# SiLU written into its PSUM bank, and GpSimd making the rests of divided down products, in a cross-attention and mixture-of-experts kernel

## The reference

```python
# x (8, 256, 128), ctx (8, 256, 96), float32; D = 128, 8 experts + 1 shared, top 2
x = x + xattn(layernorm(x), ctx)         # sim = q k^T, normalised over the whole (q, k) plane of a batch,
                                         # softmax over k, times value, times Wo^T
h = layernorm(x)
probs = softmax(h @ gate_w + gate_b); topk_probs, topk_idx = top_k(probs, 2)
cw = sum(one_hot(topk_idx, 8) * topk_probs[..., None], axis=2)
def swiglu(v): a, b = split(v, 2); return silu(a) * b
shared = swiglu(h @ sw1 + sb1) @ sw2 + sb2
routed = sum_e cw[..., e] * (swiglu(h @ rw1[e] + rb1[e]) @ rw2[e] + rb2[e])
x = x + shared + routed
```

## Time and profile before

| | |
|---|---|
| median of 3 runs | 134.9 us (134.72 to 135.77) |
| the profiled execution | 135.15 us, its span 133.4 us |
| TensorE, VectorE, ScalarE, GpSimd busy | 96%, 81%, 64%, 18% of the span |
| granted TensorE clock | full in every slice (2.4 GHz) |

### The profile page before, as it was taken

The page is one execution under the profiler, slowest core; times in us unless marked ns, Lnnn a source line. Parts: engine busy times, 40 slices in busy tenths (PEclk is TensorE's granted clock), DMA queues, the critical chain, the costliest instruction groups (busy, mean ns, idle before and its releaser), DMA issues.

```text
span 133.4 us, 2135 instructions
## 1 busy us (share of the span) xinstructions
PE 127.5 (96%) x632; PEld 96.7 (72%) x632; DVE 107.6 (81%) x313; ACT 84.8 (64%) x165; POOL 23.9 (18%) x41
## 2 busy tenths in 40 slices
PE   7899999889999999999999999999999999999992
PEld 7677796858577776686788676598677667788871
DVE  1497788696997989999759997699697879989872
ACT  1557978996265389947653299956633987647250
POOL 7184154057700020602100020001200000000000
PEclk9999999999999999999999999999999999999999
DMA  3999400002910000098000002087000207910022
GB/s 107 304 331 269 149 7 0 0 2 86 337 59 0 0 0 2 10 296 328 0 5 0 0 0 79 18 292 332 2 0 0 79 5 182 403 44 5 0 79 79
DMA packets 8828, 12.97 MB, mean 97 GB/s; under 512 B 1321, under 2 KB 6994, under 8 KB 8306
## 3 DMA queue, kind: packets, MB, share of 16 engines
q1 hardware_dynamic: 8242, 12.62, 28.1%
q10 hardware_dynamic: 576, 0.23, 0.6%
HBM read 11.73 MB, written 1.11 MB: 96 GB/s over the span
## 4 chain that ended last, share of the span: by engine, by line
PE 61%; issue 15%; DVE 9%; ACT 7%; POOL 6%; DVEq 0%; POOLq 0%; ACTq 0%
PE bank L998 55%; ACT prob L508 3%; POOL w_rest L434 3%; POOL ln_rstd L419 2%; PE bank L1062 1%; PE bank L1014 1%; ACT L553 1%; PE bank L1113 1%; PE bank L1090 1%; DVE x L902 1%; ACT act_head L580 1%; PE bank L1181 1%; DVE g_beats L824 1%; DVE g_rank L827 1%; ACT silu L588 1%
## 5 line engine op out<-in xcount | busy, mean ns | idle before, releaser
L588 ACT ACTIVATE silu<-bank,b_cols 128x512 f32<-128x512 f32 (+1 forms) x37 | 24.8, 676 | 23.7 <-PE bank L998 23.2
L998 PE MATMUL bank<-x_head,w_head 128*128 128x512 f32 x72 | 33.7, 468 | 0.3 <-issue 0.3
L998 PE MATMUL bank<-x_head,w_rest 128*128 128x512 f32 x72 | 28.5, 395 | 0.0
L998 PE MATMUL bank<-x_rest,w_head 128*128 128x512 f32 x72 | 28.5, 395 | 0.0
L881 DVE SCALAR_TENSOR_TENSOR act<-bank,b_cols,silu 128x512 f32<-128x512 f32 (+1 forms) x34 | 24.9, 734 | 1.3 <-DVE silu L873 0.3
L873 DVE TENSOR_TENSOR silu<-silu,cw_all 128x512 f32<-128x512 f32 (+1 forms) x28 | 18.6, 668 | 3.3 <-ACT silu L588 2.6
L998 PE MATMUL bank<-act,w_sb 128*128 128x512 f32 x38 | 19.4, 592 | 0.0
L998 PEld LDWEIGHTS bank<-x_head,w_head 128*128 128x128 f32 x72 | 13.6, 189 | 5.3 <-issue 2.7
L998 PEld LDWEIGHTS bank<-x_rest,w_head 128*128 128x128 f32 x72 | 13.6, 189 | 3.9 <-issue 1.9
L998 PEld LDWEIGHTS bank<-x_head,w_rest 128*128 128x128 f32 x72 | 13.5, 188 | 3.3
L890 DVE TENSOR_TENSOR act_rest<-act,act_head 128x512 fp32r<-128x512 f32 x15 | 10.0, 685 | 4.1 <-ACT silu L588 2.0
(11 more groups left out here) (130 smaller groups left out, 219.4 us busy)
## 6 DMA issues: line engine op xcount, KB each, us to landing
cw_all<-cw_dram SPq DMA_DIRECT2D x4, 1024.0 KB, 7.0
cw_all<-cw_dram SPq DMA_DIRECT2D x4, 512.0 KB, 5.0
cw_all<-cw_dram SPq DMA_DIRECT2D x6, 256.0 KB, 3.7
x_sb<-in_x_dram SPq DMA_DIRECT2D x4, 256.0 KB, 4.2
w_sb<-in_L_ffn_rw_dram SPq DMA_DIRECT2D x1, 1024.0 KB, 7.4
ctx_sb<-in_ctx_dram SPq DMA_DIRECT2D x4, 192.0 KB, 4.2
out_dram<-x SPq DMA_DIRECT2D x3, 256.0 KB, 2.1
w_sb<-in_L_ffn_rw_dram SPq DMA_DIRECT2D x1, 512.0 KB, 7.1
```

The costliest lines, as they stand in the source:

```text
L588: scalar.activation(silu[:, k, cols], hid(n, 0)[:, cols], ACT.Silu, bias=b1_cols[:, 0, e:e + 1]).then_inc(silu_sb, 1)
L998: return pe.matmul(dst, lhs, rhs, start=start, stop=stop, skip_group_check=True)
```

## The change

- SiLU of stages 4 to 8, and of stages with e >= 2 in the later chunks but the last stage, is written back into the PSUM bank that it was read from (in_bank); the weighting reads it there and writes the SBUF tile. TensorE's a half of stage n then waits for the weighting of stage n - 2, and no longer for its SiLU only. In the first routed expert of chunks 1 to 3, the b half times SiLU is written into its own bank, and the weighting reads that.
- The divided stages become 25: 4, 6, 7, 8; 9 to 13, 15, 16, 17; 18, 20, 21, 22, 24, 25, 26; 27 to 32 as before. Ten are new: 4, 6, 7, 12, 13, 15, 20, 21, 22, 24.
- For the 19 of them below 27, GpSimd makes the rest, in two instructions of 256 columns each. Before some of them it waits for a piece of VectorE's work (clear_of_vector). The six others stay on VectorE.
- Their heads are made in stage m + 2 ahead of that stage's SiLU; those of stages 7, 16 and 25 inside cw_copy, between cw_rows and cw_t.
- w2's heads are made in stage 2, w2's rests on GpSimd in stage 3. The first variance's power moves two slots later, the scores' power one slot and place.

```diff
-        POOL_AT = {'first_rstd': [-9, 1], 'scores_rstd': [-2, 0], 'second_rstd': [4, 0]}
+        POOL_AT = {'first_rstd': [-7, 1], 'scores_rstd': [-1, 1], 'second_rstd': [4, 0]}
...
+        DIVIDED_OF = [(4, 6, 7, 8), (0, 1, 2, 3, 4, 6, 7, 8), (0, 2, 3, 4, 6, 7, 8), range(NX - STRAIGHT - 1)]
+        DIVIDED = [n for n in range(NX * C) if n % NX in DIVIDED_OF[n // NX]]
+        BY_POOL = [n for n in DIVIDED if n < NX * (C - 1)]
+        BY_DVE = [n for n in DIVIDED if n not in BY_POOL]
+        WITH_WEIGHTS = [m for m in DIVIDED if m < NX * (C - 1) and m % NX == E - 1]
...
+            return m + 2 if m < NX * (C - 1) else m + 1
...
+        def in_bank(n):
+            return FOUR_BANKS_FROM <= n < LAST and n % NX >= (1 if n < NX else 2)
...
+            def clear_of_vector(m):
+                c, e = m // NX, m % NX
+                if e in (1, 2):
+                    pool.wait_ge(shift_sb, c + 2)
+                elif e == 4 and c + 2 < C:
+                    pool.wait_ge(simstat_sb, c + 3)
+                elif e == 4:
+                    pool.wait_ge(gz_sb, C)
+                elif e == 6:
+                    pool.wait_ge(cw_sb, c + 2)
+
+            def act_rests(m):
+                pool.wait_ge(act_head_sb, divided(m))
+                for cols in (slice(0, N // 2), slice(N // 2, N)):
+                    pool.tensor_tensor(act_rest[:, m % 3, cols], act[:, m % 4, cols], act_head[:, m % 3, cols].bitcast(F32), ALU.subtract).then_inc(pool_rest_sb, 1)
...
+                if n == 3:
+                    pool.wait_ge(shift_sb, 2)
+                    pool.wait_ge(scaled_sb, weighted(n))
+                    w2_rests()
+                if n - 1 in BY_POOL:
+                    clear_of_vector(n - 1)
+                    act_rests(n - 1)
...
+                    if NX * c - 2 in WITH_WEIGHTS:
+                        act_heads(NX * c - 2)
...
-                    scalar.activation(silu[:, k, cols], hid(n, 0)[:, cols], ACT.Silu, bias=b1_cols[:, 0, e:e + 1]).then_inc(silu_sb, 1)
+                    silu_out = hid(n, 0)[:, cols] if in_bank(n) else silu[:, k, cols]
+                    scalar.activation(silu_out, hid(n, 0)[:, cols], ACT.Silu, bias=b1_cols[:, 0, e:e + 1]).then_inc(silu_sb, 1)
...
-                for m in divided_in(n, ("first",)):
+                for m in heads_in(n, True):
                     act_heads(m)
                 if n >= 2:
                     expert_silu(c, e)
...
-                if n in (5, 6):
-                    w2_heads(n - 5)
+                if n == 2:
+                    w2_heads(0)
+                    w2_heads(1)
...
-                        dve.tensor_tensor(silu[:, k, cols], silu[:, k, cols], cw_all[:, e - 1, cols], ALU.mult).then_inc(scaled_sb, 1)
+                        dve.tensor_tensor(silu[:, k, cols], hid(n, 0)[:, cols] if in_bank(n) else silu[:, k, cols], cw_all[:, e - 1, cols], ALU.mult).then_inc(scaled_sb, 1)
...
-                    for m in divided_in(n, ("first", "between")):
+                    for m in dve_rests_in(n):
                         act_rests(m)
...
-                    pe.wait_ge(silu_sb, n - 1)
+                    if in_bank(n - 2):
+                        pe.wait_ge(scaled_sb, weighted(n - 2))
+                    else:
+                        pe.wait_ge(silu_sb, n - 1)
...
-                    pe.wait_ge(w2_rest_sb, 1)
-                    pe.wait_ge(act_rest_sb, divided(n))
+                    pe.wait_ge(w2_rest_sb, len(W2_GROUPS))
+                    if n in BY_POOL:
+                        pe.wait_ge(pool_rest_sb, 2 * (BY_POOL.index(n) + 1))
+                    else:
+                        pe.wait_ge(act_rest_sb, BY_DVE.index(n) + 1)
```

More of the change, by code:

```diff
@@ L307, in xattn_moe_kernel, with heads_in, dve_rests_in, weighted @@
         DOWN_BEHIND, CLOSE_FROM = 3, NX * (C - 1) + 1
-        DIVIDED = [n for n in range(NX - 1, LAST - STRAIGHT)
-                   if n >= NX * (C - 1) or n % NX in ((0, 1, 2, 7, 8) if n < NX * 2 else (0, 7, 8))]
-        def parts_slot(m):
[L313 to L323, removed]
+        DIVIDED_OF = [(4, 6, 7, 8), (0, 1, 2, 3, 4, 6, 7, 8), (0, 2, 3, 4, 6, 7, 8), range(NX - STRAIGHT - 1)]
[3 more added lines that the diff above has]
+        WITH_WEIGHTS = [m for m in DIVIDED if m < NX * (C - 1) and m % NX == E - 1]
+        def parts_slot(m):
+            return m + 2 if m < NX * (C - 1) else m + 1
+        def heads_in(n, ahead):
+            return [m for m in DIVIDED if parts_slot(m) == n and ahead == (m < NX * (C - 1)) and m not in WITH_WEIGHTS]
+        def dve_rests_in(n):
+            return [m for m in BY_DVE if parts_slot(m) == n]
+        def weighted(n):
+            c, e = n // NX, n % NX
+            return E * c + e - c
+        def in_bank(n):
+            return FOUR_BANKS_FROM <= n < LAST and n % NX >= (1 if n < NX else 2)
         def downs_in(n):
@@ L553, in router_exp, with act_heads @@
                 scalar.activation(g_exp[:, :, :], g_z[:, :, :], ACT.Exp).then_inc(gexp_sb, 1)
+            def act_heads(n):
+                scalar.wait_ge(act_sb, n + 1)
+                scalar.wait_ge(y_ps, n - 2)
+                copy(act_head[:, n % 3, :], act[:, n % 4, :]).then_inc(act_head_sb, 1)
             def cw_copy(c):
@@ L575, in w2_heads @@
                 copy(w2_head[:, lo:hi, :], w2_sb[:, lo:hi, :]).then_inc(w2_head_sb, 1)
[L577 to L580, removed]
             def expert_silu(c, e):
@@ L666, in _ @@
                     expert_silu(c, e)
-                for m in divided_in(n, ("between",)):
+                for m in heads_in(n, False):
                     act_heads(m)
@@ L856, in first_expert_gate @@
                 dve.wait_ge(b_ps, n + 1)
+                dve.scalar_tensor_tensor(hid(n, 1)[:, :], hid(n, 1)[:, :], b1_cols[:, 1, 1:2], silu[:, k, :], ALU.add, ALU.mult).then_inc(raw_act_sb, 1)
+                between()
                 dve.wait_ge(y_ps, n - 3)
-                dve.scalar_tensor_tensor(act[:, n % 4, :], hid(n, 1)[:, :], b1_cols[:, 1, 1:2], silu[:, k, :], ALU.add, ALU.mult).then_inc(raw_act_sb, 1)
-                between()
                 dve.wait_ge(cw_in[cw_group(1)], 16 * arrivals(c, cw_group(1)))
                 dve.wait_ge(raw_act_sb, c)
-                dve.tensor_tensor(act[:, n % 4, :], act[:, n % 4, :], cw_all[:, 0, :], ALU.mult).then_inc(act_sb, 1)
+                dve.tensor_tensor(act[:, n % 4, :], hid(n, 1)[:, :], cw_all[:, 0, :], ALU.mult).then_inc(act_sb, 1)
             def expert_gate(c, e, between):
@@ L876, in expert_gate @@
                     if e >= 1:
[L877 removed]
+                        dve.wait_ge(scaled_sb, weighted(n) + h)
                     dve.wait_ge(b_ps, n + 1)
@@ L985, in _ @@
                     expert_gate(c, e, between)
-                for m in divided_in(n, ("last",)):
-                    act_rests(m)
                 if n == 0:
                     first_statistics(2)
-                if n == NX:
-                    w2_rests()
                 run(n, 2)
```

11 lines of the change are left out of this document (5 added, 6 removed).

## The result

The changed kernel took 135.96 us (135.54 to 137.71, 20 runs) where the kernel before took 135.42 beside it (134.72 to 137.46, 20 runs). The ratio is 1.0052 [1.0036, 1.0067], so 0.7 us slower; it is formed only from executions in the faster of the two states that occur, and the medians of all of them differ by 0.54. The forecast was 135.4 against the earlier median of 134.9, a step of +0.5.

The account below looks back on a forecast made before the run. TensorE bounds most of the kernel, ScalarE or VectorE some stretches. Delays of 0.93 by the last router less 0.48 saved made 0.45 us slower: 135.6, or 135.4 against the 134.9 median; range 133.1 to 136.6, the forecast's own 134.7 to 136.0.

Parts of the forecast that it names:

- One divided product: Matmuls on TensorE: 0.86 us straight, 0.70 divided, so 0.16 saved each and 1.6 at best for ten.
- Edits at nothing: Moving w2's heads and rests, SiLU into its bank, and GpSimd's new waits and moved powers: costed at nothing.
- Step 1: Stages 8 to 10 (51 to 57 us): head 6 delays SiLU 8, product 7 waits for its rest; plus 0.67.
- Step 2: Stages 14 to 17 (71 to 81 us): VectorE last, savings of 12 and 13 lost, hold taken as 0; shift 0.57.
- the rival's condition: Stage 14: first moments' product, at 73.25, starts before the second half of rest 12 is over (72.45 to 73.9).
- Step 3: Stages 17 to 19 (82 to 87 us): head 15 delays SiLU 17, product 16 waits for its rest; 0.58 in all.
- Step 4: Stages 22 to 24 (94 to 100 us): VectorE late, head 20 before SiLU 22, last router starts late; 0.93 against before.
- Step 5: Products 21, 22 and 24, where TensorE is fed: 3 x 0.16 = 0.48 us gained, nothing changing after.
- The forecast case: Whole kernel: delays of the steps less the late savings, 0.45 us slower, 135.4 us; chance 0.36.
- rival B: Stage 14: GpSimd's rest 12 holds up VectorE's moments' product, 0.6 to 1.43 us, giving 136.4; chance 0.19.
- A: Whole kernel: all ten savings land, TensorE alone decides; 134.9 - 1.6 = 133.3 us; chance 0.27.
- C: Half of the delays covered as VectorE catches up, steps 3 and 4 cost nothing; 134.6 us; chance 0.12.

Follow-up runs that it names:

- bank alone: SiLU written into its bank as the only change to the kernel before; ratio to the kernel before 0.9988 [0.9974, 1.0002].
- the guard: Changed kernel, but GpSimd makes the rests of stages 12 and 21 only after the last chunk's moments' products; ratio to the kernel before 1.0018 [1.0003, 1.0033].

## Why the prediction was right, and where it was wrong

**One divided product, 0.16.** Right where TensorE is fed: from stage 24 to 28 the shift goes from 1.00 to 0.54 for three products, 0.46 against 0.48.

**Edits at nothing.** The wait on the weighting costs nothing (bank alone, no shift to stage 20). In the changed kernel it does bite once, by 0.25 before the first half of stage 10. The cover that the prediction named held there: act 8 ends at 55.63, and the second half, which had to wait for act 8 in any case, starts at 55.71 right behind the first. So it adds nothing to the delay of step 1; the gap only stands one half earlier. No gap of TensorE after is traced to a power on GpSimd. The moves of w2's work and of the powers were not run alone.

**Step 1, +0.67 forecast, 0.57 measured** at stage 11. The mechanism is shown: with no head ahead of SiLU 8 the shift is 0.06. The working was 0.10 too high: SiLU into the bank takes 0.66 where 0.69 was taken, and the head ahead of the table load moves SiLU by 0.48 (53.46 - 52.78 - 0.20) where 0.54 was taken.

**Step 2 is the step that failed.** I took the hold of the moments' product as 0, by a row of the same operation beside a GpSimd power, and kept 1.43 as the other end. It is 0.45 (0.62 - 0.17), shown by the guard. The row did not decide: the power works on 8 columns for 1.64 us, while the rest streams 256 columns through its 0.73, and the product came 1.04 us into the power. The same operation on VectorE was the wrong kind of nearness; the other party was what had to be alike. The Trainium skill (SBUF — State Buffer, Who interferes with whom) states the exclusion without that distinction. The trace agrees for the rests in both directions: VectorE is held (1.23 for a weighting, 0.62 for the moments' product), and GpSimd is held (3.27 for four halves where four take 2.83). For a power it agrees in one direction alone. Row 9.91 of the earlier trace rows speaks against a hold of VectorE, while the same kind of power waits for a weighting that came 0.17 before it, 2.02 us where it took 1.64; GpSimd in the kernel before:

```profile
53.73 2.02 POOL L410 TENSOR_TENSOR row_powers<-ln_veps,powers 128x8 f32<-128x8 f32 x1 [5.73 <-DVE ln_veps L714]
```

With the rival's condition I was right (the two met at 73.23, forecast 73.25). Its price of 0.6 to 1.43 was too high: 0.60 of the second half was left, but the product's own 0.17 passes almost whole inside that wait, so 0.45 was lost.

**Step 3, 0.58 forecast, 0.65 measured**, but with the hold in it. Between stages 16 and 20 the forecast says +0.01 and the changed kernel shows -0.17, the guarded one also -0.17. From SiLU 16 to product 16 it is 87.53 - 77.99 = 9.54 us, where it was 86.69 - 76.98 = 9.71; head and SiLU were again shorter than I took them (SiLU 17 moves by 0.47 against SiLU 16, not 0.54), and head 16 (85.27) starts 0.09 before cw_rows ends, where the sum set them end to end. The gap before product 16 stands there, as forecast. What step 3 overlooked, and the run with four new products shows, is that without head 15 the earlier head 16 and GpSimd's rest close a gap that was there before.

**Step 4, 0.93 forecast, 1.00 measured**; from the stage before, +0.35 forecast and +0.35 measured. The gap before the router is shown, and undoing product 20 alone takes it away.

**Step 5 and the sum.** 0.45 forecast, 0.42 measured by the profile (0.7 by the timed runs, with 0.2 of the 0.6 in the span there at stage 0). The total owes something to luck. The guarded kernel, without the hold, ends at -0.01, so the steps that excluded the hold were together 0.46 too high: 0.11 by stage 11, 0.08 more by stage 16, 0.18 by stage 20 and 0.10 behind stage 24. The hold, put at 0, made up for it. The forecast case was half of what happened and rival B's mechanism the other half.

**The other rivals.** A falls: of the ten savings only those of 21, 22 and 24 reach the end of the changed kernel, and leaving six products straight makes it 1.5% faster (0.9905 against 1.0052). C falls too: the delays at stages 11 and 24 were not covered at all.

## What to carry to other kernels

Before an engine's work is cut, sort the stages by who is last, and put the cut only where that engine is; the same edit at the other stages costs what it adds elsewhere (with four new products the kernel took 1.3 us less than before, with ten 0.5 to 0.7 more). A price for two engines meeting at one memory must be taken from a row where both instructions are of the kind that will meet. A slow engine can still be the right one when it is idle, as long as its input comes early enough; check what its longer duration asks of the step ahead of it.

## What the runs showed of the hardware that was not expected

- A VectorE operation with two SBUF inputs that arrives while GpSimd streams a subtraction is held to the end of that instruction. The moments' product ends 0.02 to 0.03 us after it in seven kernels: 73.85 after 73.83 in the changed one, 73.84 after 73.82 in one piece. A held weighting of 128x512 ends 0.54 to 0.55 us after it, seven times in the kernel with SiLU in SBUF, such as 101.59 after 101.04. The other way about, four GpSimd halves take 3.27 us beside a weighting out of SBUF, where four take 2.83 in the guarded kernel.
- A GpSimd power on 8 columns (8.87 to 10.51) did not hold the same VectorE operation at all, nor did it in any of the thirteen other traces, where the product begins 1.04 to 1.45 us into the power. Whether this is the operation, its 8 columns, or that the product comes late in it, was not tried; a product near the start of a power would tell.
- SiLU of 128x512 takes 659 ns into a bank and 690 into SBUF. The Trainium skill (ScalarE: Activation LUTs, Step-by-step: what each stage is for) says that ScalarE reaches PSUM faster; the trace agrees, with 0.03 us.
- GpSimd's subtraction takes 0.74 us for 256 columns and 1.28 for 512, so half a tile costs more than half: two halves in a row take 1.43.
